# Feed-forward blocks of a four-block transformer kernel: head join one tile later, halves instead of wholes, and inverse norms from logarithm, exponential and one Newton step

## What is computed

```python
x = x + attn_a(layernorm(x)); x = x + ffn(layernorm(x))
x = x + attn_b(layernorm(x)); x = x + ffn(layernorm(x))

def _layer(x, ...):                    # ffn() runs two of these (DEPTH = 2)
    q, k, v = split(shift_token(x) @ wqkv)      # 8 heads of 64
    q = l2norm(q) * qs; k = l2norm(k) * ksc     # t / clip(norm(t), 1e-12)
    q, k = rotary_xpos(q, k)
    o = local_attention(q, k, v)       # each token sees 64 back, softmax
    x = x + o @ wo
    h = layernorm(shift_token(x)) * lg + lb     # shift: right half of the
    a, g = split(h @ w1 + b1)                   # columns one token down
    return x + (a * gelu(g)) @ w2 + b2          # hidden width 341
```

## Time and profile before

| | |
|---|---|
| median of three runs | 5035.15 us |
| profiled execution | 5039.37 us, its span 5037.7 us |
| TensorE / VectorE / ScalarE / GpSimd busy | 79% / 57% / 52% / 34% of the span |
| mean granted TensorE clock | 0.864 of full speed |
| first feed-forward call, first projection to last addition to y | about 1274 to 2147 us |
| second feed-forward call | about 4150 to 5024 us |

### The profile page before, as it was taken

The page is one execution under the profiler, slowest core; times in us unless marked ns, Lnnn a source line. Parts: engine busy times, 40 slices in busy tenths (PEclk is TensorE's granted clock), DMA queues, the critical chain, the costliest instruction groups (busy, mean ns, idle before and its releaser), DMA issues.

```text
span 5037.7 us, 101534 instructions
## 1 busy us (share of the span) xinstructions
PE 3958.2 (79%) x31924; PEld 2425.0 (48%) x31924; DVE 2871.0 (57%) x5889; ACT 2620.8 (52%) x6422; POOL 1703.7 (34%) x1415
## 2 busy tenths in 40 slices
PE   2999999996688888744666664999999917888886
PEld 1555555553455555522222222777777715555554
DVE  2555555555566676543444443666666656767664
ACT  1555555553566666423333332666666605666664
POOL 0000000000777777523222221111111128777773
PEclk9999999998899999865555555999999959999998
DMA  3222222221101101017999999777777611111111
GB/s 122 78 79 82 78 79 78 84 77 45 44 22 23 24 23 23 16 66 287 382 381 378 381 379 370 260 243 273 242 275 243 227 34 26 23 23 23 23 24 28
DMA packets 373723, 701.02 MB, mean 139 GB/s; under 512 B 53220, under 2 KB 160056, under 8 KB 373608
## 3 DMA queue, kind: packets, MB, share of 16 engines
q1 hardware_dynamic: 329576, 565.25, 32.8%
q0 software_dynamic: 44032, 134.30, 7.3%
HBM read 336.53 MB, written 314.64 MB: 129 GB/s over the span
## 4 chain that ended last, share of the span: by engine, by line
PE 60%; DMA 13%; DVE 7%; issue 7%; POOL 5%; ACT 3%; SPq 1%; DVEq 1%; POOLq 0%; ACTq 0%
DMA rel_k<-b_stage_k 12%; PE ps L332 5%; PE ps L1452 5%; PE ps L340 5%; PE ps L351 5%; PE ps L1461 5%; PE ps L862 4%; PE ps L1443 3%; PE ps L821 3%; PE ps L1472 3%; PE ps L882 2%; PE ps L836 2%; PE ps L847 2%; POOL f_rn L759 2%; PE ps L1344 2%
## 5 line engine op out<-in xcount | busy, mean ns | idle before, releaser
L1368 DVE COPY b_stage_k<-ps 128x640 f32<-128x640 f32 (+2 forms) x512 | 359.3, 722 | 471.1 <-DMA rel_k<-b_stage_k 412.3
L430 ACT ACTIVATE a_p<-a_s,a_min 128x512 f32<-128x512 f32 x512 | 367.1, 718 | 469.6 <-DVE a_min L474 469.6
L1365 ACT ACTIVATE b_stage_q<-ps 128x640 f32<-128x640 f32 (+2 forms) x512 | 316.4, 624 | 506.8 <-PE ps L1347 390.2
L474 DVE CUSTOM_DVE_ANT_0 a_s<-ps,a_table 128x512 f32<-128x512 f32 x512 | 333.5, 689 | 374.4 <-PE ps L332 371.8
L1526 ACT ACTIVATE c_p<-c_s,c_min 128x512 f32<-128x512 f32 x512 | 371.0, 725 | 291.9 <-PE ps L1461 179.8
L1344 PE MATMUL ps<-b_e,b_st_k 48*128 48x512 bf16 (+1 forms) x512 | 305.9, 597 | 263.8 <-DVE b_stage_k L1368 263.8
L1561 DVE CUSTOM_DVE_ANT_0 c_s<-ps,c_rq 128x512 f32<-128x512 f32 x512 | 353.2, 690 | 202.5 <-PE ps L1452 189.8
L188 POOL COPY y<-ln_rows 128x512 f32 x32 | 19.9, 621 | 1305.2 <-DVE ln_rows L180 1305.2
L757 POOL TENSOR_TENSOR f_rot<-f_rc,f_rs 128x1024 f32<-128x1024 f32 x128 | 302.9, 2367 | 354.3 <-DVE f_rs L1017 354.0
L942 ACT ACTIVATE f_p<-f_s,f_min 128x128 f32<-128x128 f32 x1024 | 397.6, 392 | 39.6 <-DVE f_min L1005 35.6
L759 POOL TENSOR_TENSOR f_rn<-f_ss,f_power 128x16 f32<-128x16 f32 x128 | 373.8, 2920 | 14.3 <-DVE f_ss L1026 0.4
(11 more groups left out here) (171 smaller groups left out, 9374.7 us busy)
## 6 DMA issues: line engine op xcount, KB each, us to landing
rel_q<-b_stage_q SPq DMA_DIRECT2D x64, 1280.0 KB, 7.7
rel_k<-b_stage_k SPq DMA_DIRECT2D x64, 1280.0 KB, 7.7
c_rq<-rel_q SPq DMA_DIRECT2D x64, 1024.0 KB, 7.3
c_rk<-rel_k POOLq DMA_DIRECT2D x64, 1024.0 KB, 11.8
a_table<-skew_bias SPq DMA_DIRECT2D x64, 896.0 KB, 4.6
f_vb<-f_v SPq DMA_DIRECT2D x256, 128.0 KB, 2.3
rel_k<-b_stage_k SPq DMA_DIRECT2D x32, 1024.0 KB, 9.4
rel_q<-b_stage_q SPq DMA_DIRECT2D x32, 1024.0 KB, 5.3
```

The costliest lines, as they stand in the source:

```text
L430: nc.scalar.activation(a_p[:, lt % 2, h, :], a_s[:, lt % 2, h, :], ACT.Exp, bias=a_min[:, lt % 2, h:h + 1], scale=-1.0, accum_out=a_sum[:, ...
L1368: moves_b1(dve, 1, lambda out, src: nc.vector.tensor_copy(out, src))
```

## The change

- The join of the heads leaves the step of tile c and is done one step later (new argument `d`, four tiles back), behind the projection of v, into bank MIXED. The addition to y moves with it, ahead of VectorE's sum of squares.
- q and k are squared and turned separately, in halves of 512 columns, and each transpose waits for its own half.
- In step m = 2 ScalarE's first four exponentials stand behind the copies of f_qT and f_kT.
- The token shift is issued in m = 3, at the head of SP's step, and now brings whole rows; the left half is then put right by a copy on VectorE in place of one on GpSimd. VectorE's statistics stand behind the reciprocal.
- GpSimd's bias addition moves from m = 0 to m = 1.
- The power of -0.5 on GpSimd (f_rn) is replaced: ScalarE takes Ln and then Exp with scale -0.5 of the 128x16 sums, ahead of its last four exponentials, and GpSimd refines the guess with one Newton step of four small instructions. The layer norm's power (L743) stays.

```diff
@@ pool_ffn step
-                hold(pool, f_shift_loaded, 32 * (mlp.g + 2))
+            if m == 1 and mlp is not None:
                 hold(pool, f_h_left, upto_b(mlp.g))
...
-            if m == 3 and ln is not None:
-                hold(pool, f_x_mid, upto(ln.g * LT + 3))
-                hold(pool, f_hn_ready, upto_b(ln.g - 1, LT))
-                nc.gpsimd.tensor_copy(f_h[:, :, 0:DIM // 2], y[:, bass.ts(ln.y, LT), 0:DIM // 2]).then_inc(f_h_left, 1)
             if a is not None:
-                pool.wait_ge(f_turned, upto(a.g, 3))
+                pool.wait_ge(f_turned, upto(a.g, 6))
                 pool.wait_ge(f_normed, upto(a.g - 1))
                 tt(f_rot[:, :], f_rc[:, :], f_rs[:, :], ALU.add).then_inc(f_rotated, 1)
-                pool.wait_ge(f_ss_ready, upto(a.g))
-                tt(f_rn[:, :], f_ss[:, 1, :], f_power[:, :], ALU.pow).then_inc(f_rn_ready, 1)
+                pool.wait_ge(f_guessed, upto(a.g))
+                done = upto(a.g - 1, 4)
+                tt(f_nw[:, 0, :], f_guess[:, :], f_guess[:, :], ALU.mult).then_inc(f_rn_step, 1)
+                pool.wait_ge(f_rn_step, done + 1)
+                tt(f_nw[:, 1, :], f_nw[:, 0, :], f_ss[:, 1, :], ALU.mult).then_inc(f_rn_step, 1)
+                hold(pool, f_rn_step, done + 2)
+                nc.gpsimd.tensor_scalar(f_nw[:, 2, :], f_nw[:, 1, :], -0.5, 1.5, ALU.mult, ALU.add).then_inc(f_rn_step, 1)
+                pool.wait_ge(f_rn_step, done + 3)
+                tt(f_rn[:, :], f_guess[:, :], f_nw[:, 2, :], ALU.mult).then_inc(f_rn_step, 1)
@@ scalar_ffn step
-                nc.scalar.activation(f_sq[:, :], ps[:, QK:QK + 2, :].rearrange("p b n -> p (b n)"),
-                                     ACT.Square).then_inc(f_squared, 1)
+                for k in range(2):
+                    act.wait_ge(f_qk_full, upto(a.g - 1, 2) + k + 1)
+                    nc.scalar.activation(f_sq[:, k * INNER:(k + 1) * INNER], ps[:, QK + k, :],
+                                         ACT.Square).then_inc(f_squared, 1)
...
-            if s2 is not None:
+            if s2 is not None and m != 2:
                 exps(s2, 0)
...
+            if s2 is not None and m == 2:
+                exps(s2, 0)
...
+            if a is not None:
+                act.wait_ge(f_ss_ready, upto(a.g))
+                nc.scalar.activation(f_log[:, :], f_ss[:, 1, :], ACT.Ln).then_inc(f_logged, 1)
+                act.wait_ge(f_logged, upto(a.g))
+                act.wait_ge(f_rn_step, upto(a.g - 1, 4))
+                nc.scalar.activation(f_guess[:, :], f_log[:, :], ACT.Exp, scale=-0.5).then_inc(f_guessed, 1)
             if s2 is not None:
                 exps(s2, 1)
@@ tensor_ffn
         def project_v(a, h):
-            pe.wait_ge(f_x_mid, upto(a.g - 4))
-            if a.first:
-                pe.wait_ge(f_v_moved, upto(a.g - 1))
+            pe.wait_ge(f_v_moved, upto(a.g - 1))
...
-            for k, full in enumerate((f_qT_full, f_kT_full)):
+            for k, (full, moved) in enumerate(((f_qT_full, f_qT_moved), (f_kT_full, f_kT_moved))):
+                if a is not None:
+                    pe.wait_ge(f_squared, upto(a.g - 1, 2) + k + 1)
+                    pe.wait_ge(f_turned, upto(a.g - 1, 6) + 3 * k + 3)
...
+        def join_heads(m, d, mlp):
+            if m == 0 and mlp is not None:
+                pe.wait_ge(f_y_done, upto_b(mlp.g - 1))
+            if m == 1 and mlp is not None:
+                pe.wait_ge(f_hnT_moved, upto_b(mlp.g))
+            if m == 2 and mlp is not None:
+                pe.wait_ge(f_gelued, upto_b(mlp.g, 3))
+            if m == 3 and mlp is not None:
+                pe.wait_ge(f_hid_ready, upto_b(mlp.g, 3))
+            pe.wait_ge(f_oT_moved, upto(d.g))
             for i in range(PAIRS_F):
-                last = mm(ps[:, V_BANK, 0:DIM], f_oT[:, i * P:(i + 1) * P], f_wo[:, c.layer, i, :],
+                last = mm(ps[:, MIXED, 0:DIM], f_oT[:, i * P:(i + 1) * P], f_wo[:, d.layer, i, :],
...
         def mix_values(c):
...
-            pe.wait_ge(f_oT_moved, upto(c.g - 1))
+            pe.wait_ge(f_x_mid, upto(c.g - 1))
@@ tensor_ffn step
                 project_v(a, h)
+            if d is not None:
+                join_heads(m, d, mlp)
...
-            if c is not None:
-                join_heads(a, c)
@@ vector_ffn
+            for k in range(2):
...
+                dve.wait_ge(f_squared, upto(a.g - 1, 2) + k + 1)
+                tt(rc, heads, cs[:, 0, k, :].unsqueeze(1).broadcast_to([P, HF, DF]), ALU.mult).then_inc(f_turned, 1)
+                for h in range(2):
+                    to, src = slice(h * 32, h * 32 + 32), slice((1 - h) * 32, (1 - h) * 32 + 32)
+                    tt(rs[:, :, to], heads[:, :, src],
+                       cs[:, 1, k, to].unsqueeze(1).broadcast_to([P, HF, 32]), ALU.mult).then_inc(f_turned, 1)
...
         def statistics(ln):
+            hold(dve, f_shift_loaded, 32 * (ln.g + 2))
+            nc.vector.tensor_copy(f_h[:, :, 0:DIM // 2], y[:, bass.ts(ln.y, LT), 0:DIM // 2]).then_inc(f_h_left, 1)
@@ vector_ffn step
+            if d is not None:
+                dve.wait_ge(f_out_full, upto(d.g))
+                tt(y[:, d.t, :], y[:, d.t, :], ps[:, MIXED, 0:DIM], ALU.add).then_inc(f_x_mid, 1)
             if a is not None:
                 sum_squares(a)
...
-            if m == 3 and ln is not None:
-                statistics(ln)
             if s2 is not None:
...
                 nc.vector.reciprocal(f_rsum[:, s2.par, :], f_sum[:, s2.par, :]).then_inc(f_inverted, 1)
...
+            if m == 3 and ln is not None:
+                statistics(ln)
@@ sync_ffn step
+            if m == 3 and ln is not None:
+                half = slice(DIM // 2, DIM)
+                hold(sp, f_x_mid, upto(d.g))
+                hold(sp, f_hn_ready, upto_b(ln.g - 1, LT))
+                rows = y[:, bass.ts(ln.y, LT), :]
+                sp.dma_start(f_h[1:P, :, :], rows[0:P - 1, :, :]).then_inc(f_shift_loaded, 16)
+                sp.dma_start(f_h[0:1, 1:LT, half], rows[P - 1:P, 0:LT - 1, half]).then_inc(f_shift_loaded, 16)
```

More of the change, by code:

```diff
@@ L553, in program @@
     f_rn = sb("f_rn", [P, 16])
+    f_log = sb("f_log", [P, 16])
+    f_guess = sb("f_guess", [P, 16])
+    f_nw = sb("f_nw", [P, 3, 16])
     f_rc = sb("f_rc", [P, 2 * INNER])
@@ L654, in body @@
             for m in range(LT):
-                step(m, rows(0, m), rows(1, m), rows(2, m), rows(3, m), whole(-1), whole(-2), whole(1))
+                step(m, rows(0, m), rows(1, m), rows(2, m), rows(3, m), rows(4, m), whole(-1), whole(-2), whole(1))
         body(0, 0)
@@ L692, in sync_ffn, with step @@
         sp.wait_ge(f_zeros, F_ZEROS * (call + 1))
-        def step(m, a, b, s2, c, ln, mlp, nxt):
+        def step(m, a, b, s2, c, d, ln, mlp, nxt):
+            if m == 3 and ln is not None:
[5 more added lines that the diff above has]
+                sp.dma_start(f_h[0:1, 1:LT, half], rows[P - 1:P, 0:LT - 1, half]).then_inc(f_shift_loaded, 16)
             if a is not None:
@@ L700, in step @@
                 sp.dma_start(f_vb[0:WINDOW, (m + 1) % LT, :], f_v[WINDOW:P, m, :]).then_inc(f_vb_loaded[m], 16)
[L701 to L707, removed]
         ffn_loop(sp, call, step)
@@ L826, in transpose_qk @@
         def transpose_qk(a, b):
[L827 to L832, removed]
-            pe.wait_ge(f_normed, upto(b.g))
-            for k, full in enumerate((f_qT_full, f_kT_full)):
+            pe.wait_ge(f_normed, upto(b.g))
+            for k, (full, moved) in enumerate(((f_qT_full, f_qT_moved), (f_kT_full, f_kT_moved))):
+                if a is not None:
+                    pe.wait_ge(f_squared, upto(a.g - 1, 2) + k + 1)
+                    pe.wait_ge(f_turned, upto(a.g - 1, 6) + 3 * k + 3)
+                else:
+                    pe.wait_ge(moved, upto(b.g - 1))
                 for i in range(PAIRS_F):
@@ L838, in transpose_qk, with mixed_free, turn_normed @@
                 last.then_inc(full, 1)
[L840 to L845, removed]
+        def join_heads(m, d, mlp):
[8 more added lines that the diff above has]
+            pe.wait_ge(f_oT_moved, upto(d.g))
             for i in range(PAIRS_F):
-                last = mm(ps[:, V_BANK, 0:DIM], f_oT[:, i * P:(i + 1) * P], f_wo[:, c.layer, i, :],
+                last = mm(ps[:, MIXED, 0:DIM], f_oT[:, i * P:(i + 1) * P], f_wo[:, d.layer, i, :],
                           start=(i == 0), stop=(i == PAIRS_F - 1))
             last.then_inc(f_out_full, 1)
-        def turn_normed(c, mlp):
-            if c is None:
-                pe.wait_ge(f_y_done, upto_b(mlp.g - 1))
+        def mixed_free(c, d):
+            if c is not None:
+                pe.wait_ge(f_oT_moved, upto(c.g))
+            elif d is not None:
+                pe.wait_ge(f_x_mid, upto(d.g))
+        def turn_normed(c, d, mlp):
+            mixed_free(c, d)
+            pe.wait_ge(f_y_done, upto_b(mlp.g - 1))
             pe.wait_ge(f_hn_ready, upto_b(mlp.g, LT))
@@ L1010, in turn_heads @@
```

(11 more changed lines are left out.)

33 lines of the change are left out of this document (15 added, 18 removed).

## The result

The changed kernel takes 5525.02 us (median of four runs, 5513.06 to 5529.54) against 5034.88 us: a ratio of 1.097, with a 95% interval of 1.095 to 1.099. The forecast was slower, 5265 us, range 5170 to 5400: the direction is right, the loss is 490 us and not 230.

A forecast was written before the change was run, and what follows sets the result against it. No engine is full; a ring of waits sets each batch. Four tiles of 12.60 us make 50.4, plus 8.0, 0.5 clock and 0.4 long batches: 59.3 against 51.84 us; +115 per call, two calls, 5265 us, range 5170 to 5400.

The forecast's parts named there:

- part 4: Shift, statistics and moves: shift lands 4.5 us after issue (bounds 3 and 10.5), hidden; statistics and copy add 1.9 us per batch.
- the shift still takes 10.5 us: Rival: whole rows go out in as many pieces, VectorE waits about 3 us more per batch; 5365 us, chance 0.07.
- The loads: ScalarE's table loads at Ln and at its Exp: two added per tile, 1.31 us each, delaying the last four exponentials.
- the ring: Waits from VectorE's reciprocal to the next, through TensorE and ScalarE, forecast to set the pace: 12.60 us per tile.
- The plain step: One tile's step, reciprocal to reciprocal, without the batch's single additions: 12.60 us, two table loads included.
- the step with the statistics: VectorE's once-per-batch work: statistics and left-half copy add 1.9 us (0.35 + 1.55), addition of the MLP 0.7.
- the one with f_hid: The step holding the MLP product f_hid, forecast to add 2.0 us once per batch.
- mix until the copy of f_oT starts: Term from mix to ScalarE's copy of f_oT, taken as 1.25 us per tile.
- The rule on the drain: Skill page's drain of about 1380 ns per ScalarE table switch, 2.66 us per added load; the forecast used 1.31.
- The rival with one set: One ScalarE table set serves Ln and Exp, loads stay two per batch; 4930 us (4890 to 4970), chance 0.10.
- GpSimd's Newton: Four 128x16 instructions on GpSimd in place of the power: 1.1 us in all, bounds 0.4 and 4.0.
- GpSimd taking over the ring: Rival: Newton, product and probabilities on GpSimd set the pace; about 5350 us, chance 0.05 of more than 40 us.

The follow-up runs named there:

- experiment 3: The changed kernel with the power of -0.5 back on GpSimd and the shift DMA cut into 112 and 15 partitions: 4936.69 us, ratio 0.9809.
- experiment 2: The changed kernel with its shift DMA cut into 112 and 15 partitions, Ln, Exp and their loads kept: 5339.95 us, ratio 1.0609.
- experiment 4: The changed kernel with the shift cut into 112 and 15 partitions and one table set for Ln and Exp loaded: 4959.24 us, ratio 0.9850.
- experiment 1: The changed kernel with the power of -0.5 back on GpSimd, without Ln, Exp and Newton, shift uncut: 5221.02 us, ratio 1.0374.

## Why the prediction was wrong

**The step that failed is the shift in part 4**: "Whole rows are contiguous, as those of f_vb are. I take 4.5 us". What sets the time above all is how many engines share the transfer: cut in two, the whole rows land 3.7 us after issue (1547.88 to 1551.53 in experiment 3), uncut 14.1. The size of the pieces matters less: on one engine 256-byte pieces went at 16 GB/s and 2-KB pieces at 25. The forecast read the 6.88 us in the queue as the cost of small pieces. And f_vb's transfers, its model for contiguous rows, are over 64 partitions, not 127. It was in reach that the pieces were not the cost: windows of the old trace show 15 to 18 GB/s and a share of 0.07 to 0.08 from 1970 to 1977. The Trainium skill states the rule, "DMA: Bandwidth & Descriptors", section "Why a DMA increments its semaphore by 16 and not by 1": the number of engines is the largest one up to 16 that divides the outermost sizes, and 127 partitions go to one. The runs agree: a share of 0.07 for 127, 0.45 and more once it is cut. The forecast did not draw on it. The step cost 185 us of the 490 (experiment 2), and without the loads it would have been 284. The rival *the shift still takes 10.5 us* named the right place with a chance of 0.07, but its 96 us were too few (and 5265 + 96 is 5361, not 5365): twice the bytes made it 14.1 us, which leaves 6.7 us uncovered per batch, not 3.

**The loads: the mechanism was right, the sum around them too small.** Two per tile came, on the ring, as forecast. With the shift out of the way (experiment 2) the time is 5340 us, 75 above the forecast. The reciprocals of one batch there:

```profile
1746.99 0.20 DVE L1094 RECIPROCAL f_rsum<-f_sum 128x8 f32<-128x8 f32 x1 [5.08 <-ACT f_p L958]
...
1763.81 0.20 DVE L1094 RECIPROCAL f_rsum<-f_sum 128x8 f32<-128x8 f32 x1 [4.19 <-ACT f_p L958]
...
1776.70 0.20 DVE L1094 RECIPROCAL f_rsum<-f_sum 128x8 f32<-128x8 f32 x1 [5.32 <-ACT f_p L958]
...
1792.49 0.20 DVE L1094 RECIPROCAL f_rsum<-f_sum 128x8 f32<-128x8 f32 x1 [7.07 <-ACT f_p L958]
...
1808.13 0.20 DVE L1094 RECIPROCAL f_rsum<-f_sum 128x8 f32<-128x8 f32 x1 [6.06 <-ACT f_p L958]
```

The steps are 16.82, 12.89, 15.79 and 15.64 us; the sum of the forecast, by the same steps, 15.2, 12.6, 16.0 and 14.6, with 0.5 more for the clock somewhere. The plain step and Gelu's are right within 0.3 us. Short were the step with the statistics (1.6) and the one with f_hid (1.0). In the first, copy, statistics and the MLP's addition hold VectorE 3.92 us (1747.21 to 1751.13) where the forecast had 2.6; 1.3 of that are the copy that VectorE took over from GpSimd, costed at 0.35: it lasts 1.62 us. In the f_hid step the term "mix until the copy of f_oT starts", 1.25 us in the forecast and 1.24 in the plain step (1770.16 to 1771.40), takes 2.08 (1800.75 to 1802.83); the granted clock is 0.50 there and 1.00 in the plain step. So the clock costs 0.8 us in this one step, where the forecast had allowed 0.5 for the batch; TensorE's busy time per batch is 46.6 us against 40.7 in experiment 3. Why the clock stays low there no run tests.

**The rule on the drain** (the Trainium skill, "ScalarE: Activation LUTs", section "What ACT_TABLE_LOAD costs", 2.66 us for a switch) stays without support: the activation starts 0.01 us behind its load in the traces, and the 256 loads of the tiles cost 297 to 381 us, 1.16 to 1.49 each, where 2.66 would make 681.

**The rival with one set** did not happen, since the choice fell on different sets. Had it, its forecast of 4930 with a fast shift compares with 4959 measured in experiment 4. The Trainium skill, "ScalarE: Activation LUTs", section "Table sets: the hidden batching unit", says that one set holds both; experiment 4 agrees, with two loads per batch.

**The reordering** was costed well: batch 48.8 us forecast without added loads, with Ln, Exp and Newton; 49.1 to 50.1 in experiment 4, which has them, and 47.5 to 49.9 in experiment 3, which has the power. **GpSimd's Newton**: four instructions and their waits 1.3 us (1933.54 to 1934.83), 1.1 forecast. **GpSimd taking over the ring** was given little chance, and in one step of the changed kernel it did release TensorE last: the guess came at 1933.46, Newton, product and probabilities followed without a gap, and TensorE transposed at 1938.64. That reciprocal-to-reciprocal step was 13.68 us, not 12.60, but at a granted clock of 0.88; the same step of experiment 2, at 1.00 and with the same wait of 1.76 us for the probabilities, took 12.89. So some 0.3 us of it can be put down to GpSimd. TensorE's waits for the turned q and k fell as forecast, from 142 us between 1300 and 2100 us to 52.

**The costs do not add.** Loads, Ln, Exp and Newton together cost 304 us with the late shift and 403 with the cut one (experiment 2 less 3); the shift costs 185 us with the loads and 284 without. Each hides some 100 us of the other: where the loads delay the reciprocal, the shift is waited for less, 227 us in the changed kernel against 328 in experiment 1. 304 + 284 - 98 (the gain of the order) = 490 is the whole change.

## What to carry to other kernels

Before a function that the kernel has not used goes to ScalarE, ask which table set it will be served from and what stands behind the load; two loads of 1.28 us per tile undid an order that gains 2% by itself, and naming the common set by hand took the cost away. A transfer's time is read from its DMA share and GB/s in a window, and not guessed from its bytes or from its time in the queue: 127 partitions rode on one engine of sixteen, 112 and 15 did not. When a transfer is issued a step later, its old landing time, hidden until then, must be laid against what still covers it.

## What was unexpected of the hardware

VectorE's copy from SBUF to SBUF of 128x256 takes 0.29 us in the changed kernel, 1.5 us on average in experiment 2 and, in single cases, up to 2.03 in experiment 3. In experiment 2 it starts while GpSimd runs its product, and ends 0.15 us behind it (1869.68 + 1.90 = 1871.58, 1870.10 + 1.63 = 1871.73):

```profile
1870.10 1.63 DVE L1056 COPY f_h<-y 128x256 f32<-128x256 f32 x1
```

```profile
1869.68 1.90 POOL L771 TENSOR_TENSOR f_qk<-f_rot,f_rn 128x1024 f32<-128x1024 f32 x1
```

The Trainium skill, "SBUF — State Buffer", section "Who interferes with whom", says that a copy in a mode that uses both of VectorE's port pairs and a GpSimd instruction take the shared pair in turn, the one issued first for its whole length. The rows agree; the mode of the copy no trace names. In the changed kernel the late shift itself had moved the copy past GpSimd's work.
